# A bidirectional decay scan written as one fp32 product per channel with its matrix of lag weights, and the second layer norm moved behind all channels

## What is computed

```python
def step(carry, xt):              # one direction; w, u: one value per channel
    A, Bd = carry                 # the carry before step t is the output of step t
    ekt, vt = xt                  # ek = exp(k), k = v = ctx
    return (ew * A + ekt * vt, ew * Bd + ekt), (A, Bd)
...
cur = exp(u + k)
wkv = (Af + Ab + cur * v) / (Bf + Bb + cur)
x = x + tanh(g_xattn) * sigmoid(layernorm(x)) * wkv
x = x + tanh(g_ffn) * ffn(layernorm(x))   # ffn: int8 grid with one scale for the whole tensor
```

## Time and profile before

| | us |
|---|---|
| median of 3 runs | 244.47 |
| lowest and highest | 243.53, 245.61 |
| profiled execution, its span from first to last instruction | 242.7 |
| busy DVE, ACT, PE, POOL in it | 219.1, 166.9, 160.8, 121.4 |
| bytes read from and written to HBM | 10.75 MB, 4.19 MB |

### The profile page before, as it was taken

How to read it: one execution, slowest core, us unless ns; L and a number is a source line. 1 busy time by engine, 2 the same in 40 slices (tenths; PEclk the granted TensorE clock), 3 DMA queues, 4 the chain that set the end, 5 groups by cost and what they waited for, 6 DMA issues and landing times.

```text
span 242.7 us, 3539 instructions
## 1 busy us (share of the span) xinstructions
PE 160.8 (66%) x1006; PEld 118.8 (49%) x1006; DVE 219.1 (90%) x307; ACT 166.9 (69%) x220; POOL 121.4 (50%) x151
## 2 busy tenths in 40 slices
PE   0608665468946569568463932999595994789970
PEld 0408565458936469458453821533232342566640
DVE  0999999999999999999999787379999998899993
ACT  5454975929959286594781759999797886689700
POOL 7431444438455394354742750057373773008992
PEclk9999979996879967797998665799999997599995
DMA  5696666610000000000000000000000000002358
GB/s 151 217 339 202 181 224 208 214 44 4 0 0 0 0 0 0 0 0 0 0 0 0 4 0 0 0 1 0 3 0 0 0 0 0 1 3 86 130 185 293
DMA packets 16108, 15.10 MB, mean 62 GB/s; under 512 B 2016, under 2 KB 15840, under 8 KB 16096
## 3 DMA queue, kind: packets, MB, share of 16 engines
q1 hardware_dynamic: 16096, 14.95, 19.3%
HBM read 10.75 MB, written 4.19 MB: 62 GB/s over the span
## 4 chain that ended last, share of the span: by engine, by line
DVE 31%; issue 21%; PE 18%; ACT 14%; POOL 10%; DVEq 2%; DMA 2%; POOLq 0%; SPq 0%; ACTq 0%
DVE hidden L666 9%; PE ps L1015 8%; PE ps L979 6%; DVE hidden L664 3%; POOL x_all L334 3%; POOL rs L357 3%; ACT silu_out L567 2%; DVE h_space L824 2%; ACT h_space L567 2%; DVE hidden L779 2%; DVE h_peaks L790 2%; DMA hidden<-in_ctx 2%; DVE bn L623 1%; DVE x L767 1%; DVE w_scale L611 1%
## 5 line engine op out<-in xcount | busy, mean ns | idle before, releaser
L882 PE MATMUL ps<-ident,hidden 128*128 128x128 f32 x128 | 42.1, 329 | 46.7 <-POOL hidden L325 20.2
L882 PEld LDWEIGHTS ps<-ident,hidden 128*128 128x128 f32 x128 | 21.4, 167 | 53.2 <-POOL hidden L325 42.3
L884 PE MATMUL ps<-ident,hidden 128*128 128x128 f32 x128 | 41.0, 320 | 0.0
L886 PE MATMUL ps<-ident,hidden 128*128 128x128 f32 x128 | 40.9, 319 | 0.0
L664 DVE TENSOR_TENSOR_SCAN hidden<-hidden,ps 128x1024 f32<-128x1024 f32 x16 | 36.3, 2270 | 0.0
L666 DVE TENSOR_TENSOR_SCAN hidden<-xq,ps 128x1024 f32<-128x1024 f32 x16 | 36.2, 2262 | 0.0
L325 POOL TENSOR_TENSOR hidden<-zero_tile 128x18 f32<-128x18 f32 x16 | 3.5, 222 | 56.7 <-DVE hidden L666 56.7
L443 ACT ACTIVATE hidden<-hidden 128x512 f32<-128x512 f32 x16 | 10.0, 626 | 31.4 <-DVE hidden L677 31.3
L979 PE MATMUL ps<-xq,wuT 128*128 128x512 bf16 (+1 forms) x96 | 23.3, 384 | 6.5 <-DVE hidden L779 6.2
L790 DVE TENSOR_REDUCE h_peaks<-hidden (+2 forms) x24 | 26.1, 1122 | 0.8 <-POOL hidden L387 0.5
L1015 PE MATMUL ps<-wdT,z_t 128*128 128x256 bf16 (+1 forms) x192 | 25.2, 287 | 2.0 <-ACT z_t L585 2.0
(11 more groups left out here) (93 smaller groups left out, 371.3 us busy)
## 6 DMA issues: line engine op xcount, KB each, us to landing
hidden<-in_ctx SPq DMA_DIRECT2D x8, 512.0 KB, 3.7
x_all<-in_x SPq DMA_DIRECT2D x8, 512.0 KB, 4.6
out<-x_all SPq DMA_DIRECT2D x16, 256.0 KB, 2.2
h_space<-in_L_ffn_w_down SPq DMA_DIRECT2D x1, 704.0 KB, 6.6
z_t<-in_L_ffn_w_gate SPq DMA_DIRECT2D x1, 640.0 KB, 6.3
z_t<-in_L_ffn_w_up SPq DMA_DIRECT2D x1, 640.0 KB, 7.5
z_t<-in_L_ffn_w_gate SPq DMA_DIRECT2D x2, 64.0 KB, 6.5
z_t<-in_L_ffn_w_up SPq DMA_DIRECT2D x2, 64.0 KB, 6.9
```

The source lines that it names most:

```text
L882: nc.tensor.matmul(dst, cur[:, h, q, i * T:(i + 1) * T], ident[:, :], start=True, stop=False, is_transpose=True)
L884: nc.tensor.matmul(dst, scans[:, h, 0, q * UNIT + i * T:q * UNIT + (i + 1) * T], ident[:, :], start=False, stop=False, is_transpose=True)
L886: last = nc.tensor.matmul(dst, scans[:, h, 1, q * UNIT + i * T + 1:q * UNIT + (i + 1) * T + 1], ident[:, :], start=False, stop=True, is_tr ...
```

## The change

Channels are no longer transposed and scanned. For one channel, the sum over both directions and the step itself is a product with a 128x128 matrix whose element (s, t) depends on the lag |t - s| alone: exp(w(|t - s| - 1)) off the diagonal, exp(u) on it. ACT computes the 255 lag weights of each channel on 32 partitions with 8 channels side by side (`lag_weights`), and stores them twice to a scratch tensor in HBM, 2 x 261 KB (row of 8 x 255 values per 8 channels). For each of 32 chunks of 8 channels SP then loads a 128 x 1,024 tile, 512 KB (`load_lags`): partition s takes the 1,024 contiguous values that begin 8 values (32 B) before those of partition s - 1, so the rows overlap. Partitions 0 to 63 read the first copy, 64 to 127 the second. PE multiplies each channel's matrix, fp32 without transpose flag, by that channel's 32 columns of ek and 32 of pk (`accumulate`), which lie side by side 256 values apart; 8 channels fill one bank, with a step of 8. There are 6 slots for lag tiles and 6 banks.

DVE forms denominators and mixes per chunk (256 columns); ACT's reciprocals and POOL's residuals go by pairs of chunks. As a chunk covers all sequences, exp(-z) of all groups has to be there before the first denominator, and all channels are needed before any statistics of the second norm are whole: DVE takes those of channels 0 to 127 early (`early_stats`), those of 128 to 255 behind the last residual (`late_stats`), then come `rstd2`, `normalise`, PE's transposes, `keep_z` and `peak_z` for all 8 groups. The products ek * ctx are shared by DVE (5 groups) and POOL (3). The down weights are now also cast and turned among the chunks. From the global peak on the code is that of before.

```diff
@@ SP
+            def load_lags(j):
+                if j >= SLOTS:
+                    sp.wait_ge(s["ab_done"], j - SLOTS + 1)
+                src = bass.AP(lag_dram, j * CG * LAGS + CG * (T - 1),
+                              [[LG * CG * LAGS - CG * T // 2, 2], [-CG, T // 2], [1, CG * T]])
+                sp.dma_start(lag_tile[j % SLOTS].rearrange("p t i -> p (t i)"), src) \
+                    .then_inc(lag_in[j % SLOTS], 16)
...
-            with sp.Fori(2, GROUPS) as g:
-                next_load(g)
+            for g in range(GROUPS):
+                load_ctx(g)
+            sp.wait_ge(s["lag_stored"], 32)
+            load_lags(0)
+            load_lags(1)
+            load_x(0)
...
+            for j in range(SLOTS, CHUNKS):
+                load_lags(j)
+                if j == SLOTS + 1:
+                    load_weights(1)
+                if j == CHUNKS // 2:
+                    load_weights(2)
@@ ACT
+            def lag_weights():
...
+                for i in range(CG):
+                    nc.scalar.activation(lag_w[0:LG, :, i], lag_row[0:LG, :], ACT.Exp, scale=wu[:, i:i + 1]) \
+                        .then_inc(s["lag_done"], 1)
...
+                for copy in range(2):
+                    act.dma_start(lag_dram[copy, :, :], lag_w[0:LG, :, :].rearrange("p j i -> p (j i)")).then_inc(s["lag_stored"], 16)
...
+            normalise(0)
+            for g in range(1, GROUPS):
+                normalise(g)
+                keep_z(g - 1)
@@ DVE
-            def scan(g, h):
...
-                nc.vector.tensor_tensor_scan(scans[:, h, 0, 1:2 * UNIT + 1], decay[0][:, h, :], src, 0.0,
-                                             ALU.mult, ALU.add)
...
+            def late_stats(g):
+
+                dve.wait_ge(s["x1_done"], PAIRS)
                 for i in range(GS):
+                    last = stats2(g * GS + i, 1)
...
+            def denominator(j):
+
+                dve.wait_ge(s["ab_done"], j + 1)
+                if j == 0:
+                    dve.wait_ge(s["ez_done"], GROUPS)
@@ PE
+            def accumulate(j):
+
+                pe.wait_ge(lag_in[j % SLOTS], 16 * (j // SLOTS + 1))
+                if j == 0:
+                    pe.wait_ge(s["pk_dve"], len(DVE_GROUPS))
+                    pe.wait_ge(s["pk_pool"], len(POOL_GROUPS))
+                wait(pe, s["mix_done"], j - BANKS + 1)
+                for c in range(CK):
+                    last = nc.tensor.matmul(ps[:, j % BANKS, c:2 * HALF:CK], lag_tile[j % SLOTS][:, :, c],
+                                            ekp[:, j * CK + c:2 * SEQS * C:C], start=True, stop=True)
+                last.then_inc(s["ab_done"], 1)
```

More of the change, by code:

```diff
@@ new lines, in gated_rwkv_ffn @@
+        at = 2 * SEQS * C
+        lag_tile = [hidden[:, at + i * CK * T:at + (i + 1) * CK * T].rearrange("p (t i) -> p t i", i=CG)
+                    for i in range(SLOTS)]
+        assert at + SLOTS * CK * T <= BLOCKS * HB
+        z_all = hidden[:, 0:SEQS * C]
+        z_flat = z_t[:, :, :].rearrange("p h n -> p (h n)")
+        ez = z_flat
+        late = silu_out[:, :, :].rearrange("p s n -> p (s n)")
+        den = h8_space[:, WC:WC + 2 * 512].rearrange("p (s n) -> p s n", s=2)
+        rden = late[:, 0:2 * 512].rearrange("p (s n) -> p s n", s=2)
@@ L146, in gated_rwkv_ffn @@
         pool_sums = [n for n in range(SUMS) if n not in dve_sums]
+        POOL_GROUPS = 1, 3, 5
+        DVE_GROUPS = [g for g in range(GROUPS) if g not in POOL_GROUPS]
         names = ["g_x", "g_f", "clx", "cld", "tanh_x", "tanh_f", "sgx", "sgd", "s_x", "inv_x", "s_h", "inv_h",
@@ L203, in gated_rwkv_ffn, with channels @@
         out_v = out.rearrange("b t c -> t b c")
[L205 to L215, removed]
-            for g in range(end, stop or GROUPS + last_skew):
-                step(g)
-        def do_early(early, g, h):
-            for work, m in early.get((g, h), ()) if isinstance(g, int) else ():
-                work(m)
         def seqs(tile, first, n):
-            return tile[:, bass.ds(first * C, n * C)].rearrange("p (b c) -> p b c", c=C)
+            return tile[:, first * C:(first + n) * C].rearrange("p (b c) -> p b c", c=C)
+        def channels(tile, first, n):
+            return tile.rearrange("p (b c) -> p b c", c=C)[:, :, first:first + n]
         @block.sync
@@ L263, in _ @@
-            load_values("g_x", g_xattn)
-            load_ctx(0)
-            with nc.allow_non_contiguous_dma("256 values, once"):
-                for i, src in enumerate((w, u)):
-                    sp.dma_start(wu_raw[:, 2 * i:2 * i + 2],
-                                 src.rearrange("a b (h c) -> c (a b h)", h=CH)).then_inc(s["wu_in"], 16)
-            load_x(0)
+                    sp.wait_ge(s["w_quant"], 1)
+                    sp.dma_start(down[:, :, 0:I], src).then_inc(weights_in[m], 16)
@@ new lines, in load_weights @@
+                    sp.dma_start(down[:, :, I:KA * P], src[:, :, KI * P:I]).then_inc(weights_in[m], 16)
+            with nc.allow_non_contiguous_dma("256 values, once"):
+                sp.dma_start(wu[:, 0:CG], w.rearrange("a b (p i) -> p (a b i)", i=CG)).then_inc(s["w_in"], 16)
+                sp.dma_start(wu[:, CG:2 * CG], u.rearrange("a b (p i) -> p (a b i)", i=CG)).then_inc(s["u_in"], 16)
+            load_values("g_x", g_xattn)
+            for g in range(GROUPS):
+                load_ctx(g)
@@ L381, in _ @@
+            for g in range(GROUPS):
+                rstd1(g)
+            for m in range(PAIRS):
+                residual(m)
+            for g in range(GROUPS):
+                rstd2(g)
             with pool.Fori(0, BLOCKS // 2) as pair:
@@ L642, in stats2, with early_stats @@
+            def early_stats(first, n):
+                dve.wait_ge(s["x1_done"], PAIRS // 2)
+                for i in range(first, first + n):
+                    stats2(i, 0)
+            def late_stats(g):
+                dve.wait_ge(s["x1_done"], PAIRS)
                 for i in range(GS):
-                    last = nc.vector.bn_stats(bn2[:, i, :], xs[:, i, :])
+                    last = stats2(g * GS + i, 1)
                 last.then_inc(s["bn2_done"], 1)
-                wait(dve, s["bn2_done"], g + 1)
```

593 lines of the change are left out of this document (234 added, 359 removed).

## The result

The changed kernel takes 500.25 us (median of 4 runs, 499.35 to 501.75), beside 245.04 for the kernel before (4 runs on the same chip). The ratio is 2.041, 95% interval 2.032 to 2.050. The prediction was 515 us, with a range of 455 to 590. The profiled execution has a span of 498.3 us.

What follows compares the result with a forecast made beforehand. Lag loads on two DMA engines were taken to bound the kernel: landed at 382.9 us, residual done at 390.7, first gate matmul at 423.4, plus 89.7 and 1.8 gives 514.9, predicted as 515 us, range 455 to 590.

Steps and rivals of the forecast that it cites:

- Two engines: Lag loads: outermost 2 of the source leaves each load on 2 of 16 DMA engines, 10.8 us; chance 0.80.
- step 2: Load queue: 32 lag loads at 10.8 us plus 19.3 us of x and weights, last tile landed at 382.9 us.
- the sum: The forecast's five steps added along the kernel: span 513.1 us, plus 1.8 us around it, 514.9 us.
- Step 1: Kernel start: ctx loads end near 16 us; first product at about 23 us, hidden.
- Step 3: Last chunk after its load: 3.4 us of PE records, then 4.4 us to the residual, done at 390.7 us.
- Step 4: Second layer norm, now standing alone: last z at 418.0 us, then 5.4 us to the first gate matmul at 423.4.
- Step 5: From first gate matmul to the end: 89.7 us unchanged, span 513.1 us, plus 1.8 us gives 514.9.
- PE's record: Lag products on PE: 0.21 us per record at half clock, 0.107 at 2.4 GHz, 16 records per chunk.
- A: Rival for the lag loads: all sixteen engines carry them, PE just hidden; 217 us, 11% faster, chance 0.15.
- B: Rival for the chunks: sixteen engines carry loads, PE at half clock between bursts; 263 us, 8% slower, chance 0.03.
- What would show it: Signs during the lag loads: DMA share about 0.12, some 50 GB/s, PE at half clock, records every 0.21 us.
- Rival C: Lag loads on two engines slower than any row: 13.1 us a load, 588 us; upper end of the forecast's own case.

Runs made afterwards that it cites:

- filler's run: Kernel with sixteen copies of the lag weights, plus one unread bf16 matmul of 128x128 by 256 columns behind every second product: 325.5 us.

## Why the prediction was right, point by point

**Two engines (step 2): right, and shown.** The price per load was set at 10.8 us and came out at 10.1 (26 GB/s per engine in place of 24.3). The 15% that the sum added to the busiest stretch's 21.2 was an estimate; it measured 23%. Four copies halved the price; the exchange of two dimensions at equal addresses took it away (349 GB/s). The Trainium skill's rule ("DMA: Bandwidth & Descriptors", section on why a DMA increments its semaphore by 16 and not by 1) agrees with these runs (shares of 0.13, 0.28 and 1.08 for 2, 4 and 64 outermost). The estimate from its 425 GB/s, a sixteenth per engine, was 9.9 us for a load, nearer than the sum's 10.8.

**The sum, step by step.** Step 1: the first lag load was issued at 16.96 us (16). Step 2: the last tile was in place at 366.98, 382.9 predicted; first to last product of a chunk are 336.05 us, 31 x 10.08 = 312.5 for the loads; the 23.6 left over are put down to x and weights beside them (19.3). Step 3: the last chunk took 4.1 and its tail 4.1 (3.4, 4.4). Step 4: 24.8 us from residual to last z (27.3), 5.7 to the gate (5.4). Step 5: 92.6 to the end (89.7). Together 366.98 + 8.2 + 30.5 + 92.6 = 498.3. The error of 15 us is in step 2: 31 x 0.72 = 22 us too much for the loads, against 4 too little for x and weights and 2 for the first load, which was in place at 30.9 (16 + 10.8 + 2.0 = 28.8). So two errors of the step partly offset each other. The later steps nearly cancel: 3 us more for the last stage, and 2.5 less in step 4, where ACT took 21.5 us for its fifteen groups of instructions in place of 23.6. The last stage, whose code is the same, took 90.7 to 95.8 us in the profiled executions of the other variants; what moves it was not looked at. DVE, said to be far from the bound, is busy a third of the span.

**The first product (step 1) was said to be at 23 us and was at 30.9.** The kernel with the exchanged dimensions, with a fast first load, started at 25.5. The 5 us between are the first lag load on two engines. It was hidden, as said, because the loads bounded all from the start.

**PE's record was mis-sized: 0.25 us for 0.21.** The term that failed is the 0.21 us per record, taken over from the earlier trace rows, where the weights lie side by side, to weights that don't. With lag weights 8 values apart, 0.244 us were measured, and 0.213 once they were contiguous, just the value of the earlier trace rows. A rule of the Trainium skill bears on it ("SBUF — State Buffer", section on the DMA port swizzle): accesses that step past 16 bytes, 4 fp32 values, pay a penalty. The stride here is 32 bytes, and the runs agree. It cost 0.5 us in the last chunk, as all other chunks lay under their loads. The other half of the term, "half of that, 0.107, at 2.4 GHz", came from transposes. No run shows it for these products: with 128 columns of data they took 0.248 us at either level with the stride, and 0.219 at 1.00 without.

**The rivals were priced too low.** A (217) and B (263) supposed fast loads. The runs gave 291.8 at best (two copies, rows apart, fast loads) and 314.8 for the kernel that computes the layer. Against B's 263, for the first: chunks at 3.9 us in place of 3.4 (16 us), the three turns of weights stop PE for 4.6, 4.6 and 3.8 us and not for under one each (the first step between denominators is 8.49 us, in which PE waits 3.15 for ACT's cast and works 1.46; 11 us more), and a start 2.5 us later; 29 in all. B's slow pace of PE came true and its chance of 0.03 depended on the engines alone, but its reason, the clock at half between bursts, is not shown: the one strided pace that was seen at both levels didn't move with them. For A's 1.71 us per chunk there is no sign, as no run had a chunk below 3.4 us.

**What would show it.** Share 0.13 (0.12 said) and 52 GB/s (some 50 said): right. The lag loads' time to landing isn't printed on the page. "PE's clock at half there" didn't show: the row reads 1.00, and below it is told why that row may not settle it. "A PE record of L789 every 0.21 us" failed (0.25). "All engines idle over half the span" held.

**Two readings to set right.** The 62.5 us that PE is said to wait for POOL's zeroing add up the waits of L882's matmuls (20.2) and of its loads (42.3), which lie beside each other in time; before the matmuls PE is idle 46.7 us in all. Nothing in the sum hangs on it. Rival C calls 13.1 us a load "slower than any row", but the prediction's own working from the earlier trace rows gives 12.4 to 14.7 us for two engines. So the upper end of the range cut off part of what its rows allowed, and it was the measured 10.1 us that made this harmless.

## What to carry to other kernels

Look at the outermost dimension of every DMA's source as it is written, not at its size: [2, 64, 1024] and [64, 2, 1024] over the same bytes ran at 57 and 349 GB/s, and the slow one also held up what was queued behind it. Before scans become fp32 products with few columns, price the records: here 512 at 0.244 us are 125 us, more than the 72.5 us of the scans they replaced, and the second norm that lay beside the scans then stood alone for 25 us. So even sixteen engines left the kernel 28% slower than before. And an operand that all later work needs, here x for exp(-z), is best not queued between large loads: with eight and sixteen copies it was x that held back the first denominator, up to 69 us, and no longer the lag loads.

## What the runs showed that was not expected

**The granted clock reads 1.00 where PE runs at its lower pace.** In the changed kernel the clock's row is 1.00 through all chunks and up to 426 us. But its gate products begin with 4 in 1.98 us at 405.75 with the row at 1.00, and the kernel with sixteen copies has the same 1.98 us with the row at 0.50:

```profile
220.82 1.98 PE L863 MATMUL ps<-xq,wgT 128*128 128x512 bf16 x4 [2.51 <-ACT xq L500]
...
226.93 1.03 PE L863 MATMUL ps<-xq,wgT 128*128 128x512 bf16 x4
```

In the changed kernel 8 transposes of z take 1.97 us all the way (1.92 at a clock of 0.50 in the earlier trace rows), and its clock row first falls after 426 us. In the filler's run, above, a filler takes the same time on both sides of the first fall, at 157 us. The row seems to hold 1.00 until the first fall that the trace records, so before that the pace of a known group is the better gauge. That is a reading of these rows, and no run was made to settle it.

**A busy PE stayed at the lower clock.** In the filler's run the row reads 0.50 from 157 to 195 us, and PE is busy without a gap all that time (30.00 of 30.00 us in the row above). With sixteen copies PE is just as busy (20.00 of 20.00 us from 160 to 180), but there the row is at 1.00 and has not yet fallen, so its clock is not known. Its 12 weight transposes among the chunks take 1.46 us each of three times, which says little about the chunks: they come right behind a wait of 2.4 to 3.2 us, and with twice the columns of data the third set takes 1.46 us too, at a clock of 0.50, between chunks most of which are at 1.00. What a contiguous record of 64 columns costs at 1.00 is open, as no stretch at 1.00 behind a recorded fall has one.

**Issuing can take long.** The shortest issues of a lag load and of a load of x take SP 0.5 and 0.6 us. In the changed kernel a load of x behind two lag loads held SP for 8.5 us. The first three rows are of that kernel, the last of the one with the dimensions exchanged:

```profile
16.96 1.19 SPq L236 DMA_DIRECT2D hidden<-lag_w  x2
18.19 8.54 SPq L228 DMA_DIRECT2D x_all<-in_x  x1
26.77 5.60 SPq L236 DMA_DIRECT2D hidden<-lag_w  x1
...
18.54 0.60 SPq L228 DMA_DIRECT2D x_all<-in_x  x1
```

That the two engines' queues are full then is a reading of these rows; no run tests it.
